# Attention heads: probability tiles transposed row tile by row tile, with one signal per scaled tile

## The reference, cut to what matters

```python
        scores = jnp.einsum('bthd,bshd->bhts', q, k) * scale
        causal = jnp.tril(jnp.ones((T, T), bool))
        scores = jnp.where(causal[None, None], scores, -jnp.inf)
        attn = jax.nn.softmax(scores, axis=-1)
        y = jnp.einsum('bhts,bshd->bthd', attn, v).reshape(B, T, H * Dh)
        return y / 3.0 @ Wo.T
```

## Time and profile before

| | us |
|---|---|
| median of 3 runs | 1721.63 |
| lowest and highest of them | 1718.85, 1722.12 |
| the profiled execution's own time | 1727.47 |
| its span, first to last instruction | 1725.7 |
| TensorE busy in the span | 1548.3 |
| VectorE busy | 1174.9 |
| ScalarE busy | 926.7 |
| GpSimd busy | 706.0 |

### The profile page before, as it was taken

The page is one execution under the profiler, slowest core; times in us unless marked ns, Lnnn a source line. Parts: engine busy times, 40 slices in busy tenths (PEclk is TensorE's granted clock), DMA queues, the critical chain, the costliest instruction groups (busy, mean ns, idle before and its releaser), DMA issues. The chain is left out here.

```text
span 1725.7 us, 26051 instructions
## 1 busy us (share of the span) xinstructions
PE 1548.3 (90%) x8400; PEld 1218.3 (71%) x8400; DVE 1174.9 (68%) x2492; ACT 926.7 (54%) x2012; POOL 706.0 (41%) x686
## 2 busy tenths in 40 slices
PE   6999869988999898899989989879999897999898
PEld 4777658876787688745645546568887785888787
DVE  5888847775787678889979974346666444665633
ACT  5555526664665466576656542146565444565543
POOL 5999842315222233159819852112212232212222
PEclk9999979998999999999999998899999998999999
DMA  4212122102111222050023000011111212111111
GB/s 127 77 59 78 37 90 92 65 1 67 45 49 54 78 93 89 19 205 1 1 92 132 1 6 1 7 47 50 33 49 55 74 37 69 41 49 43 64 57 48
DMA packets 34333, 98.37 MB, mean 57 GB/s; under 512 B 6388, under 2 KB 11256, under 8 KB 32072
## 3 DMA queue, kind: packets, MB, share of 16 engines
q1 hardware_dynamic: 33064, 90.95, 15.8%
q0 software_dynamic: 1184, 6.37, 1.1%
HBM read 96.12 MB, written 1.18 MB: 56 GB/s over the span
## 5 line engine op out<-in xcount | busy, mean ns | idle before, releaser
L910 POOL TENSOR_TENSOR head_low<-head,head_high 128x512 fp32r<-128x512 f32 x64 | 81.8, 1278 | 460.4 <-ACT head_high L900 459.7
L1809 POOL TENSOR_TENSOR experts_low<-experts,experts_high 128x1536 fp32r<-128x1536 f32 (+1 forms) x64 | 144.6, 2263 | 285.2 <-ACT experts_high L1755 161.8
L1262 ACT ACTIVATE probs<-banks,neg_max 128x512 f32<-128x512 f32 (+3 forms) x256 | 131.4, 526 | 151.3 <-DVE neg_max L1172 151.3
L2348 POOL TENSOR_TENSOR rings<-du,bc_rows 128x512 f32<-128x512 f32 x124 | 155.3, 1271 | 20.7 <-DVE banks L2274 13.3
L2274 DVE TENSOR_TENSOR_SCAN banks<-banks,rings 128x512 f32<-128x512 f32 x128 | 156.0, 1220 | 2.6 <-ACT banks L2172 1.8
L219 PE MATMUL banks<-experts_high,xnT_high 128*128 128x384 f32 (+1 forms) x384 | 139.8, 364 | 6.1 <-POOL experts_low L1809 6.1
L1474 ACT ACTIVATE act_out<-banks 128x256 f32<-128x256 f32 (+2 forms) x112 | 47.5, 424 | 179.9 <-PE banks L219 179.6
L1506 DVE SCALAR_TENSOR_TENSOR hidden<-banks,weight,act_out 128x96 f32<-128x96 f32 (+1 forms) x192 | 62.7, 368 | 117.0 <-ACT act_out L1474 116.5
L2066 PE MATMUL banks<-rings,ident 128*128 128x512 f32 x256 | 126.5, 607 | 17.6 <-DVE rings L2297 17.2
L219 PE MATMUL banks<-experts_high,xnT_low 128*128 128x384 f32 (+1 forms) x384 | 137.8, 359 | 0.0
L219 PE MATMUL banks<-experts_low,xnT_high 128*128 128x384 f32 (+1 forms) x384 | 137.7, 359 | 0.0
(11 more groups left out here) (287 smaller groups left out, 4729.7 us busy)
## 6 DMA issues: line engine op xcount, KB each, us to landing
head<-in_heads SPq DMA_DIRECT2D x64, 384.0 KB, 3.1
experts<-in_experts SPq DMA_DIRECT2D x16, 1152.0 KB, 5.1
bc_rows<-bc_rows SPq DMA_DIRECT2D x30, 512.0 KB, 6.2
experts<-in_experts SPq DMA_DIRECT2D x16, 768.0 KB, 4.3
values<-in_values SPq DMA_DIRECT2D x32, 256.0 KB, 3.1
coef<-in_spline_coef POOLq DMA_DIRECT2D x8, 768.0 KB, 4.6
idx<-in_lut_idx SPq DMA_DIRECT2D x16, 134.0 KB, 2.1
x<-in_x SPq DMA_DIRECT2D x2, 512.0 KB, 4.4
```

Of the source, the lines that this page charges most:

```text
L1262: last = nc.scalar.activation(prob_tile(i), score_tile(i), ACT.Exp, bias=neg_max[:, i:i + 1], scale=QK_SCALE, accum_out=row_sum[:, i:i + 1])
L1809: nc.gpsimd.tensor_tensor(parts[gpar][1][:, columns], raw[gpar][:, columns], parts[gpar][0][:, columns].bitcast(FP32), ALU.subtract)\
L2348: nc.gpsimd.tensor_tensor(inflow[:, step % INFLOWS], du[:, c], B_of(n), ALU.mult)\
```

## The change

`turn` now walks the row tiles in the order in which VectorE scales them: it waits for the signal of a tile and does all of that tile's transposes. A row tile's transposes go to different banks, so no bank is complete before the last tile, and `turn` signals once, at its end. VectorE signals after each of the four scalings. ScalarE waits once and then copies the three banks one after the other. The transposes, their operands and their outputs are the same ten.

```diff
-        def turn():
-            for k in range(NT):
-                out = score_tile(3 - k)
-                for i in range(k, NT):
-                    last = nc.tensor.transpose(out[:, (i - k) * P:(i - k + 1) * P],
+        def turn(h):
+
+            for n, i in enumerate((3, 2, 1, 0)):
+
+                pe.wait_ge(probs_ready.sem, probs_ready.at(NT * h + n + 1))
+                for k in range(i + 1):
+                    last = nc.tensor.transpose(score_tile(3 - k)[:, (i - k) * P:(i - k + 1) * P],
                                                prob_tile(i)[:, k * P:(k + 1) * P], m.ident[:])
-                if k != 2:
-                    last.then_inc(turned.sem, 1)
+            last.then_inc(turned.sem, 1)
...
-
-            pe.wait_ge(probs_ready.sem, probs_ready.at(h + 1))
-            turn()
+            turn(h)
...
             for i in (3, 2, 1, 0):
-                last = nc.vector.tensor_scalar(prob_tile(i), prob_tile(i), row_inv[:, i:i + 1], None,
-                                               ALU.mult)
-            last.then_inc(probs_ready.sem, 1)
+                nc.vector.tensor_scalar(prob_tile(i), prob_tile(i), row_inv[:, i:i + 1], None, ALU.mult)\
+                  .then_inc(probs_ready.sem, 1)
...
         def store_turned(h):
+            act.wait_ge(turned.sem, turned.at(h + 1))
             for k, (at, cols) in enumerate(TURNED_BANKS):
-
-                act.wait_ge(turned.sem, turned.at(3 * h + k + 1))
                 nc.scalar.activation(probsT[:, at:at + cols], m.banks[:, k, 0:cols], ACT.Copy)\
                   .then_inc(probsT_ready.sem, 1)
```

More of the change, by code:

```diff
@@ L1340, in close @@
     def close():
-        for s, n in ((qk_projected, 2 * HEADS), (v_projected, HEADS), (scored, 3 * HEADS), (turned, 3 * HEADS),
+        for s, n in ((qk_projected, 2 * HEADS), (v_projected, HEADS), (scored, 3 * HEADS), (turned, HEADS),
                      (attended, HEADS), (added, HEADS + 1), (qk_ready, HEADS), (max_ready, HEADS), (exp_ready, HEADS),
-                     (probs_ready, HEADS), (v_ready, HEADS), (probsT_ready, 3 * HEADS), (y_ready, HEADS),
+                     (probs_ready, NT * HEADS), (v_ready, HEADS), (probsT_ready, 3 * HEADS), (y_ready, HEADS),
                      (dve_chain, HEADS * (CHAIN_QK + CHAIN_SOFTMAX))):
```

## The result

The changed kernel takes 1740.57 us (median of 6 runs, 1734.97 to 1743.42), the kernel before 1721.88 in the same comparison: a ratio of 1.0097, 95% interval 1.0076 to 1.0119. It is 18.7 us slower. The forecast was +9.5 us, with a range that ended at 1738. The sign was right; the forecast was about half the size.

What follows compares the result with a forecast made beforehand. TensorE, the busiest engine, idled 42.7 us before its transposes, mostly in pass one and the last heads. Terms 10.9 + 3.1 - 1.0 - 3.5 = +9.5 us, on the median 1731.1 us; range 1724 to 1738.

Steps and rivals of the forecast that it cites:

- Passes two to four, late copy: Middle heads: first copy waits for all ten transposes, delaying `attend`; +0.42 a head in passes three and four, +0.24 in two.
- the weight load that shows: Pass two: `attend`'s weight load, hidden before, shows by up to 0.1 us after a wait, within the 0.24 a head.
- a visible gap in TensorE's busy time: Sign for pass two: TensorE no longer busy 149.00 of 149.00 us, but a gap of 0.24 a head.
- Signals and waits at nothing: All heads: added signals and waits taken as 0, with 4.6 us as bound if no register instructions were hidden.
- 12 heads x 0.08: Pass one: next scores come at most 0.08 us earlier a head, held by VectorE's L1154; -1.0 us.
- L398 now falls between two scalings: Pass one rival: GpSimd's L398 blocks the last scaling, +1.8 us; waits or phase to the bad side together 0.15.
- I leave at nothing: Heads 0 and 14 of each pass: late copy and earlier transposes roughly cancel, within 0.3 us in all.
- 0.95 earlier: Last heads of passes three and four: `attend` starts 0.95 us earlier, 2 x 0.95 of the -3.5.
- a clock that comes back sooner: Rival, last heads of passes three and four: up to 1.5 us gained each; first pass or clock to good side 0.17.
- The other side, late copies free: Rival: the copies' late start costs nothing, only gains remain, 1711.9 us; chance 0.06.

Runs made afterwards that it cites:

- second profile of before: The kernel before run once more with no edit, for a second profiled execution: 1722.1 us, one time.
- one_wait: Changed kernel, but VectorE signals only after its last scaling and TensorE waits once, for that: 1754.72 us, 1.0172.
- first_block_by_tile: Kernel before in column-block order, but TensorE takes block 0's four transposes as their row tiles are scaled: 1717.66 us, 0.9965.
- four_signals: Kernel before, but VectorE signals after each of its four scalings and TensorE waits for the fourth: 1723.73 us, 0.9989.
- row_head15: Kernel before with row-tile order in head 15 of each pass alone, VectorE signalling every tile: 1720.26 us, 0.9986.
- last_at_once: first_block_by_tile with VectorE's copy rests moved earlier in the last layer, and last heads of passes three and four waiting for all tiles: 1711.25 us, 0.9932.
- col_one_term: Kernel before, but GpSimd makes only the first of the spline rows' terms in pass one and no L398 sums: 1701.83 us, 0.9881.

## Why the prediction was wrong in size

The table sets the forecast's terms against the passes of both profiles of the changed kernel, each less the second profile of before (us, from the starts of the `yT` copies).

| | forecast | first profile | second profile |
|---|---|---|---|
| passes three and four, head 0 to 13 | +10.9 | +13.1 | +12.7 |
| pass two, head 0 to 13 | +3.1 | +3.1 | +3.0 |
| pass one, head 0 to 13 | -1.0 | +3.5 | +3.4 |
| last heads, 13 to 15, four passes | -3.5 | -1.4 | +2.2 |
| the four passes | +9.5 | +18.3 | +21.3 |

- **Passes two to four, late copy: right.** The middle heads grew by 0.42 and 0.23 where 0.42 and 0.24 were forecast, and through the steps named: copy later, first rest behind it, `attend` behind that; the weight load that shows. `one_wait` has the late copy without the rest of the change and the same step in pass two; `first_block_by_tile` has the early start without the late copy and keeps the pace of the kernel before. The one thing that pass two didn't show is a visible gap in TensorE's busy time.
- **Signals and waits at nothing: right.** `four_signals` is 0.9989, and `one_wait` has pass two at the changed kernel's pace.
- **Pass one: wrong, the step "12 heads x 0.08".** It took one head as all, and got -1.0 where +3.5 and +3.4 were measured: half of the forecast's shortfall in the first profile, over a third in the second. (Its end of the tenth transpose, 73.49, is also off: 73.16 + 0.27 = 73.43. The term doesn't hang on it.) The earlier trace rows show a head in which L398 stood ahead of all four scalings, and there the forecast was too careful: such heads now take 0.75 less. Every other head had L398 just behind the fourth scaling, and those take 1.14 more. The rival "L398 now falls between two scalings" named this mechanism and gave it +1.8; it happened, and costs more. The term would have been wrong without L398 too: with GpSimd's further terms and sums left out nothing ends last but the copy, as in pass two, and the heads lose 0.23.
- **Head 0 of passes three and four: wrong, the step "I leave at nothing".** The step to head 1 was 0.4 where the clock stayed and 1.2 to 1.6 where it fell, in three of four cases; 0.42 of it was in the sum. The late copy makes TensorE wait 1.67 us in front of `attend` in head 0, and where the first copy was late the clock fell in 7 of 10, where it was early in 1 of 18.
- **Last heads: wrong, the step "0.95 earlier" carried to the end.** `attend` came 0.77 earlier in pass three, so the mechanism held that far. That the end would follow assumed the clock of before. Heads 13 to 15 of passes three and four together cost +1.5 in both profiles, forecast -1.9. I had the clock as a rival on the good side only, "a clock that comes back sooner"; it came back later. In the last heads of passes one and two the forecast had -1.6 together; -3.0 and +0.7 were measured, and two profiles can't settle that term.
- **The other side, late copies free:** refuted by `one_wait`.

What stays open: why the clock falls in one execution and stays in another after the same 1.67 us wait, and how much of the distance between 16 and 19 us in the medians and 18 to 21 in the profiled passes is scatter of the untouched stretches. The two profiles of the changed kernel were 2.4 and 2.3 us shorter there than the second of before; two profiles can't settle whether that is more than chance. In the last head of pass four `row_head15` speaks for the unbroken start and `last_at_once` against it; the count of 14 and 3 is all that stands between them.

## What to carry to other kernels

When a producer's tiles are consumed piece by piece, ask first what the consumer's first output needs. Here the next stage needed block 0 and all four tiles: taking the tiles in their order for block 0 alone kept the early start and the early copy (0.9965), taking all work tile by tile gave the early copy away (1.0097). Before you call a transfer the one that holds a stage, look at what the waiting engine does meanwhile: two things that end within 0.1 us of each other must both be moved (0.8 us and none in the last layer for each alone, 3.1 for both). And in a stage that alternates, read two heads, not one.

## What the runs showed of the hardware that was not expected

- An earlier start can lose by the clock. In the last head of pass three TensorE started its transposes 2.8 us before the last tile was ready (1344.00, and 1343.46 + 3.37 = 1346.83) rather than after it, stood twice for 0.7 us, and ran `attend` at 1.2 GHz (3.72 us) rather than at 2.4 (2.04 us). In the ten profiled last heads of passes three and four with row-tile order and the early start the step from head 14 took 16.40 to 16.56 us; in the twelve of column-block order with a wait for all tiles 15.5 to 15.9, twice 16.9. With the late copy and an unbroken start (`one_wait`) it took 16.26 twice, at the full clock.
- The same wait of 1.67 us was followed by half the clock in one execution and by the full clock in another of the same kernel.
- A VectorE scaling of 128 columns took 1.90 us instead of 0.50 when GpSimd's L398 (1.81 us) started within a few hundredths of a us of it. Beside GpSimd's shorter L392 it took 0.50, and 0.28 in pass one of `col_one_term`, where GpSimd stood idle.
